# Quantising the feed-forward input in two vector passes instead of three

## The chip, the cores and the metric

The kernel runs on all eight cores of one Trainium2 chip. Each core takes two of the 16 sequences (8192 tokens of 1024 features) and works alone; nothing is exchanged. The time is the device time of the slowest core, in microseconds (us).

## The reference

One layer: a state-space block, a residual and a layer norm, then a quantised feed-forward, a residual and a layer norm.

```python
def fixed_quant(x, width, frac_width):
    scale = 2.0 ** frac_width
    return clip(round(x * scale), -2 ** (width - 1), 2 ** (width - 1) - 1) / scale

x = layernorm(x + ssm(x))                       # (16, 4096, 1024), eps = 1e-5
h = einsum(fixed_quant(x, 8, 4), fixed_quant(w1, 8, 6)) + fixed_quant(b1, 8, 6)
h = relu(fixed_quant(h, 8, 4))                  # hidden size 4096
y = einsum(fixed_quant(h, 8, 4), fixed_quant(w2, 8, 6)) + fixed_quant(b2, 8, 6)
x = layernorm(x + y)
```

Activations are rounded to sixteenths and clipped to -128/16 .. 127/16; weights and biases are rounded to 64ths.

## The kernel before

Features lie on the 128 partitions, tokens along the free dimension. The instruction order of each engine is written out by hand, with a wait on a semaphore wherever a value crosses engines or a buffer comes free. Rounding is done by adding and subtracting MAGIC = 1.5 x 2^23 in float32.

**First stage** (up to some 850 us): 16 blocks of 512 tokens through the state-space block; the residual sum r1 goes to DRAM (r1s) in bfloat16.

**Weights** (some 860 to 1005 us): w1 and w2 are loaded in float32 and quantised by VectorE (DVE) into w1q and w2q in three passes of 4096 columns (L456, L460, L464).

**Feed-forward loop**: 32 blocks of 256 tokens, in a software pipeline. One iteration `it` works on three blocks: t1 = it + 1 (first layer norm LN1 and quantising of x1), t2 = it (up projection by w1) and t3 = it - 1 (down projection by w2, residual, second layer norm LN2). In the steady state TensorE (PE) does in this order:

1. LN1's column sums of r1 and of its squares for t1 (16 matmuls);
2. the down projection of t3, eight groups of 32 matmuls; after the fourth, the two broadcasts of LN1's mean and reciprocal deviation (L540, L545);
3. LN2's column sums for t3 (16 matmuls, L617 to L624), into two PSUM banks of their own;
4. the up projection of t2, 32 groups of eight matmuls; after the 28th, the broadcasts of LN2's rows.

VectorE does in this order: three short instructions on one row for LN1 (L513, L518, L523); one residual sum per down-projection group (L596); LN1 applied to eight chunks of x1 (L554 subtract, L560 multiply); the quantising of x1 into xq_sb, in two halves of four chunks with three passes each (L648, L653, L659); the row instructions for LN2 (L513, L518, L523); then for each four groups of the up projection three passes (L708 out of PSUM, L715, L723) into hq_sb; and last LN2 applied to the eight chunks of the output (L554, L560). ScalarE makes the squares (L505, L603) and, for either norm, rstd = exp(-0.5 ln(var + eps)) on a row (L529, L532).

Banks: `take_bank` deals out banks 0 to 5 in turn, and a bank taken again waits for whoever read it last; banks 6 and 7 are for the broadcasts. After LN2's sums the up projection gets four banks and then the two of the sums, which DVE frees with L513 and L523. The next down projection waits for the last L723 (`hq_vd`). A line L219 or L216 is the helper `mm_group`, which issues most matmuls (L216 the last one of a group).

Scales before the change: x1 is kept at its own scale, in float32, and multiplied by 16 in the first quantising pass; xq and hq hold integers (16 times the value), w1q and w2q hold the rounded weight over 16 (integer/1024), so that both projections come out at the value's own scale.

Of the kernel before, what the change touches and what calls it, by code (L numbers as in the profile page):

```python
# [7 lines left out]
F32 = mybir.dt.float32  # L8
BF16 = mybir.dt.bfloat16
AF = mybir.ActivationFunctionType  # L10
ALU = mybir.AluOpType
# [6 lines left out]
HID = 4096  # L18
# [8 lines left out]
MAGIC = 12582912.0  # L27
EPS = 1e-5
# [6 lines left out]
def build_nc(debug=False):  # L35
# [37 lines left out]
    def sb(name, shape, dtype, region, at=None):  # L73
        if at is None:
            off = (ptr[region] + 31) // 32 * 32
            ptr[region] = off + nbytes_pp(shape, dtype)
        else:
            off = at
        assert off + nbytes_pp(shape, dtype) <= SB_TOP, (name, off)
        h = nc.alloc_sbuf_tensor_at(name, shape, dtype, offset=off)  # L80
        handles[name] = (h, off)
        return h
# [7 lines left out]
    ones_bf = sb("ones_bf", [128, 1], BF16, "P")  # L90
    cb_one = sb("cb_one", [128, 1], F32, "P")
    cb_eps = sb("cb_eps", [128, 1], F32, "P")
    ones_row = sb("ones_row", [1, 128], F32, "P")
    rows1 = tuple(sb("row1_%d" % i, [1, 256], F32, "P") for i in range(4))
    rows2 = rows1
# [50 lines left out]
    with contextlib.ExitStack() as st:  # L146
# [27 lines left out]
        def op(eng, fn, inc=None, inck=1):  # L174
            if inc is None:
                emit(eng, fn)
                return None
            cnt[inc] += inck
            emit(eng, lambda E, f=fn, s=sems[inc], k=inck: f(E).then_inc(s, k))
            return cnt[inc]  # L180
# [64 lines left out]
        op("V", lambda E: E.memset(ones_bf[:], 1.0))  # L245
        op("V", lambda E: E.memset(ones_row[:], 1.0))
        op("V", lambda E: E.memset(cb_one[:], 1.0))
        cv = op("V", lambda E: E.memset(cb_eps[:], EPS), inc="vd")
        wait("S", "qw", qw_all)
        wait("S", "vd", cv)  # L250
        op("S", lambda E: E.activation(out=tmpc1[:], in_=vecs_sb[:, 1:2], func=AF.Exp))
# [21 lines left out]
            return v  # L273

        quant_cols(b1q16, vecs_sb[:, 10:42], 1.0 / 64.0)
        quant_cols(b2q, vecs_sb[:, 42:50], 1.0 / 64.0)
        op("V", lambda E: E.memset(ztmp8[:, 0, 0:1], 0.0), inc="vd")

        dbgA_qs = [0]
# [162 lines left out]
        wq_loads = []  # L442
        first_stage = True

        def stage_quant(dst_ap, src_ap, ncols, si, shape4=False):
            nonlocal first_stage
            pre = list(endA) if first_stage else []
            if len(wq_loads) >= 2:
                pre.append(("vd", wq_loads[-2][1]))
            first_stage = False  # L450
            stg = wstage4[si] if shape4 else wstage[si]
            qv = dma("Y", "qt%d" % si, stg[:, 0:ncols] if not shape4 else stg[:, :, :],
                     src_ap, pre=pre)
            wait("V", "qt%d" % si, qv)
            sap = stg[:, :, :] if shape4 else stg[:, 0:ncols]
            v = op("V", lambda E, s=sap: E.tensor_scalar(  # L456
                out=s, in0=s, scalar1=64.0, scalar2=MAGIC,
                op0=ALU.mult, op1=ALU.add), inc="vd")
            wait("V", "vd", v, selfdep=True)
            v = op("V", lambda E, s=sap: E.tensor_scalar(  # L460
                out=s, in0=s, scalar1=MAGIC, scalar2=127.0,
                op0=ALU.subtract, op1=ALU.min), inc="vd")
            wait("V", "vd", v, selfdep=True)
            vv = op("V", lambda E, s=sap, d=dst_ap: E.tensor_scalar(  # L464
                out=d, in0=s, scalar1=-128.0, scalar2=1.0 / 1024.0,
                op0=ALU.max, op1=ALU.mult), inc="vd")
            wq_loads.append((qv, vv))

# [4 lines left out]
        for k4 in range(HC // 4):  # L473
            stage_quant(w2q[:, 4 * k4:4 * k4 + 4, :],
                        w2T.rearrange("(k p) e -> p k e", p=128)[:, 4 * k4:4 * k4 + 4, :],
                        HID, k4 % 2, shape4=True)
        wq_done = wq_loads[-1][1]

        r1_load = [None] * NTB
# [27 lines left out]
                    inc="sd")  # L507
            state[n]["sq1_sd"] = sqv

        def rows_and_s(bm, bv, tv_m, tv_v, rows):  # L510
            mr, tr, vr, rr = rows
            wait("V", "tm", tv_m)
            vv = op("V", lambda E, b=bm, mr=mr: E.tensor_scalar(  # L513
                out=mr[0:1, :], in0=row_slice(b, TB), scalar1=1.0 / D,
                scalar2=None, op0=ALU.mult, op1=ALU.bypass), inc="vd")
            free_bank(bm, "vd", vv)
            wait("V", "vd", vv, selfdep=True)
            vv = op("V", lambda E, mr=mr, tr=tr: E.tensor_tensor(  # L518
                out=tr[0:1, :], in0=mr[0:1, :], in1=mr[0:1, :],
                op=ALU.mult), inc="vd")  # L520
            wait("V", "tm", tv_v)
            wait("V", "vd", vv, selfdep=True)
            vv = op("V", lambda E, b=bv, tr=tr, vr=vr: E.scalar_tensor_tensor(  # L523
                out=vr[0:1, :], in0=row_slice(b, TB), scalar=1.0 / D,
                in1=tr[0:1, :], op0=ALU.mult, op1=ALU.subtract), inc="vd")
            free_bank(bv, "vd", vv)
            rows_vd = vv
            wait("S", "vd", rows_vd)
            op("S", lambda E, tr=tr, vr=vr: E.activation(  # L529
                out=tr[0:1, :], in_=vr[0:1, :], func=AF.Ln, bias=cb_eps[0:1, :]))  # L530
            drn("S")
            sv = op("S", lambda E, tr=tr, rr=rr: E.activation(  # L532
                out=rr[0:1, :], in_=tr[0:1, :], func=AF.Exp, scale=-0.5), inc="sd")
            return rows_vd, sv

        def emit_bcasts(rows, rows_vd, sv):
# [28 lines left out]
        for it in range(-1, NTB + 1):  # L565
# [4 lines left out]
            if do1:  # L570
                p1 = t1 % 2
                wait("T", "qy%d" % p1, r1_load[t1])
                wait("T", "vd", wq_done)
                if "sq1_sd" not in state[t1]:
                    emit_sq1(t1)
                src1 = [r1ld[:, p1, c, :] for c in range(DC)]
                dst1 = [x1_sb[:, p1, c, :] for c in range(DC)]
                bm1, tvm1 = mm_group([(ones_bf[:], src1[c]) for c in range(DC)],
                                     lambda b: row_slice(b, TB))
                bv1, tvv1 = mm_group([(ones_bf[:], sqb1[:, c, :]) for c in range(DC)],  # L580
                                     lambda b: row_slice(b, TB),
                                     pre_waits=[("sd", state[t1]["sq1_sd"])])
                r1ld_free_T[t1] = max(tvm1, tvv1)
                rows1_vd, sv1 = rows_and_s(bm1, bv1, tvm1, tvv1, rows1)
            if do3:
                p3 = t3 % 2
                st3 = state[t3]
# [44 lines left out]
            if do1:  # L632
                if do3:
                    wait("V", "vd", r2_vd, selfdep=True)
                apply1_vd = emit_apply(src1, dst1, bmb1, brs1, tvrs1)
                r1ld_free_V[t1] = apply1_vd
                if debug and t1 == 0:
                    dma("Y", "qd", dbg["x10"].rearrange("(c p) t -> p c t", p=128),
                        x1_sb[:, 0, :, :], pre=[("vd", apply1_vd)])
                if debug and t1 == 1:  # L640
                    wait("V", "qd", cnt["qd"])
                wait("V", "vd", apply1_vd, selfdep=True)
                for half in range(2):
                    wait("V", "vd", prev_htmp_v[0], selfdep=True)
                    wait("V", "sd", prev_htmp_s[0])
                    for j in range(4):
                        c = half * 4 + j
                        v = op("V", lambda E, c=c, j=j, p=p1: E.tensor_scalar(  # L648
                            out=htmp8b[:, j, :], in0=x1_sb[:, p, c, :], scalar1=16.0,
                            scalar2=MAGIC, op0=ALU.mult, op1=ALU.add), inc="vd")  # L650
                    wait("V", "vd", v, selfdep=True)
                    for j in range(4):
                        v = op("V", lambda E, j=j: E.tensor_scalar(  # L653
                            out=htmp8b[:, j, :], in0=htmp8b[:, j, :], scalar1=MAGIC,
                            scalar2=127.0, op0=ALU.subtract, op1=ALU.min), inc="vd")
                    wait("V", "vd", v, selfdep=True)
                    for j in range(4):
                        c = half * 4 + j
                        xq_vd = op("V", lambda E, c=c, j=j, p=p1: E.tensor_scalar(  # L659
                            out=xq_sb[:, p, c, :], in0=htmp8b[:, j, :], scalar1=-128.0,  # L660
                            scalar2=None, op0=ALU.max, op1=ALU.bypass), inc="vd")
                    prev_htmp_v[0] = xq_vd
                state[t1]["xq_vd"] = xq_vd
                if t1 + 2 < NTB:
                    load_r1(t1 + 2)
            ln2_rows = [None]
            if do3:
                ln2_rows[0] = rows_and_s(bm2, bv2, tvm2, tvv2, rows2)

            def emit_ln2_rows():  # L670
                rows2_vd, sv2 = ln2_rows[0]
# [150 lines left out]
```

How the kernel before makes its waits and increments, by code:

```python
        def wait(eng, sem, val, force=False, selfdep=False):  # L161
            if val is None or val <= 0:
                return
            if not force and not selfdep and own_sem.get(eng) == sem:
                return
            if not force and waited[eng].get(sem, 0) >= val:
                return
            waited[eng][sem] = max(waited[eng].get(sem, 0), val)
            emit(eng, lambda E, s=sems[sem], v=val: E.wait_ge(s, v))
# [4 lines left out]
        def op(eng, fn, inc=None, inck=1):  # L174
            if inc is None:
                emit(eng, fn)
                return None
            cnt[inc] += inck
            emit(eng, lambda E, f=fn, s=sems[inc], k=inck: f(E).then_inc(s, k))
            return cnt[inc]
```

## Time and profile before

| | us |
|---|---|
| median of three timed runs | 3506.78 |
| lowest and highest of them | 3428.13, 3526.78 |
| the profiled execution | 3429.99 |
| its span on the slowest core (core 1) | 3428.4 |
| spans of the eight cores | 3403.0 to 3428.4 |
| PE busy with matmuls | 2869.7 (84%) |
| DVE busy | 2017.1 (59%) |
| ScalarE busy | 462.6 (13%) |

PE's busy share is high in both loops, but it counts a matmul at the lower clock as busy for twice as long, and it is an average over stretches in which PE waits for nobody and stretches in which it waits for DVE. What an edit is worth has to be read from the stretch in which it lies. The granted clock is given as a share of full speed: 1 is 2.4 GHz, 0.5 is 1.2 GHz.

### The profile page before, as it was taken

What the parts mean: (1) busy time and instruction counts of PE and PEld (TensorE: products, weight loads), DVE (VectorE), ACT (ScalarE), POOL (GpSimd) and SP (SyncE); (2) the same over time, 40 slices, a digit from 0 to 9 for tenths busy, and PEclk for the clock granted to TensorE, in tenths of its full rate; (3) what the DMA queues carried; (4) which work ended last, traced back from release to release, by engine and by line L of the source; (5) the groups of instructions that cost most, each with busy time, mean ns of one, the idle gap of its engine ahead of it and who ended that gap; (6) DMA issues with size and microseconds to landing.
All of it is one profiled execution on the core that took longest, in us unless ns stands there. A gap on an engine that the chain in (4) does not pass through costs nothing.

```text
span 3428.4 us, 55367 instructions; the slowest of 8 cores (3403.0 to 3428.4 us)
## 1 busy us (share of the span) xinstructions
PE 2869.7 (84%) x21120; PEld 2099.6 (61%) x21120; DVE 2017.1 (59%) x5836; ACT 462.6 (13%) x979; POOL 19.0 (1%) x26
## 2 busy tenths in 40 slices
PE   2999999998018888888888888888888888888888
PEld 0444444443006677777677777767777776777776
DVE  0343344344676767765777765676776666676655
ACT  0322322331000100011010011101001101100100
POOL 0000000000000000000000000000000000000000
PEclk9999999999558999999999999999999998999999
DMA  8121222120650000000000000000001000000000
GB/s 120 25 44 31 50 50 42 33 50 25 233 190 7 26 19 20 23 28 20 26 19 20 20 32 19 20 26 20 20 19 32 20 20 26 19 20 20 26 13 26
DMA packets 109811, 128.10 MB, mean 37 GB/s; under 512 B 3936, under 2 KB 102240, under 8 KB 108528
## 3 DMA queue, kind: packets, MB, share of 16 engines
q1 hardware_dynamic: 71936, 83.89, 7.4%
q0 software_dynamic: 20976, 23.89, 5.2%
q10 hardware_dynamic: 16640, 16.78, 1.8%
q8 instruction: 173, 2.83, 0.3%
q14 instruction: 86, 0.70, 0.1%
HBM read 98.07 MB, written 50.33 MB: 43 GB/s over the span
## 4 chain that ended last, share of the span: by engine, by line
PE 74%; DVE 18%; issue 2%; DMA 2%; another core or an unknown queue 2%; ACT 0%; DVEq 0%; ACTq 0%; SPq 0%
PE pb L219 65%; PE pb L216 7%; DVE x_sb L560 3%; DVE x_sb L554 3%; DVE htmp8b L708 2%; DVE htmp8b L653 2%; DVE htmp8b L648 2%; DVE xq_sb L659 2%; DVE htmp8b L715 1%; DVE hq_sb L723 1%; PE pb L540 1%; DMA wstage_b<-w2T 1%; PE pb L545 1%; DMA wstage_a<-w1T 1%
## 5 line engine op out<-in xcount | busy, mean ns | idle before, releaser
L219 PE MATMUL pb<-xq_sb,w1q 128*128 128x256 bf16 x7168 | 973.3, 286 | 218.9 <-DVE row L513 214.3
L219 PE MATMUL pb<-hq_sb,w2q 128*128 128x256 bf16 x7936 | 920.5, 277 | 72.0 <-DVE hq_sb L723 72.0
L219 PEld LDWEIGHTS pb<-xq_sb,w1q 128*128 128x128 bf16 x7168 | 726.1, 102 | 355.2 <-issue 238.4
L219 PEld LDWEIGHTS pb<-hq_sb,w2q 128*128 128x128 bf16 x7936 | 783.0, 99 | 190.3 <-issue 90.4
L596 DVE SCALAR_TENSOR_TENSOR r_sb<-pb,b2q,x_sb 128x256 bf16<-128x256 f32 x256 | 123.1, 481 | 647.6 <-PE pb L216 647.5
L219 PE MATMUL pb<-xb,winT_sb 128*128 128x512 bf16 x1792 | 435.2, 383 | 68.1 <-DMA xb<-xT 64.8
L708 DVE TENSOR_SCALAR htmp8b<-pb,b1q 128x256 f32<-128x256 f32 x1024 | 426.8, 476 | 50.7 <-DVE hq_sb L723 26.3
L219 PEld LDWEIGHTS pb<-xb,winT_sb 128*128 128x128 bf16 x1792 | 175.7, 99 | 285.1 <-issue 89.1
L216 PE MATMUL pb<-xq_sb,w1q 128*128 128x256 bf16 x1024 | 289.8, 283 | 0.0
L723 DVE TENSOR_SCALAR hq_sb<-htmp8b 128x256 bf16<-128x256 f32 x1024 | 230.6, 289 | 28.1 <-DVE htmp8b L715 0.9
L715 DVE TENSOR_SCALAR htmp8b<-htmp8b 128x256 f32<-128x256 f32 x1024 | 230.7, 289 | 27.8 <-DVE htmp8b L708 0.5
L390 DVE TENSOR_TENSOR r_sb<-pb,xb 128x512 bf16<-128x512 f32 x128 | 88.6, 692 | 243.0 <-PE pb L216 243.0
L529 ACT ACTIVATE row<-row,cb_eps 1x256 f32<-1x256 f32 x64 | 32.6, 510 | 1436.9 <-DVE row L523 1423.9
L219 PE MATMUL pb<-z_sb,woutT_sb 128*128 128x512 bf16 x896 | 215.8, 381 | 8.7 <-DVE z_sb L418 8.7
L603 ACT ACTIVATE sqb<-r_sb 128x256 bf16<-128x256 bf16 x256 | 104.4, 415 | 722.7 <-DVE r_sb L596 722.6
L219 PEld LDWEIGHTS pb<-z_sb,woutT_sb 128*128 128x128 bf16 x896 | 88.0, 98 | 115.6 <-issue 10.9
L219 PE MATMUL pb<-r1ld,ones_bf 128*1 128x256 bf16 x224 | 31.1, 281 | 145.7 <-DMA r1ld<-r1s 145.7
L342 DVE TENSOR_SCALAR ld_t<-sp_t,negrate 128x512 f32<-128x512 f32 x16 | 7.8, 486 | 229.3 <-ACT sp_t L338 229.3
L321 ACT CAST u_bf<-pb 128x512 bf16<-128x512 f32 x128 | 75.1, 587 | 398.6 <-PE pb L216 398.6
L216 PEld LDWEIGHTS pb<-xq_sb,w1q 128*128 128x128 bf16 x1024 | 104.2, 102 | 15.7
L219 PEld LDWEIGHTS pb<-r1ld,ones_bf 128*1 128x1 bf16 x224 | 16.6, 85 | 157.8 <-issue 153.2
L505 ACT ACTIVATE sqb<-r1ld 128x256 bf16<-128x256 bf16 x256 | 81.6, 401 | 185.6 <-DMA r1ld<-r1s 185.6
(93 smaller groups left out, 1855.2 us busy)
## 6 DMA issues: line engine op xcount, KB each, us to landing
outT<-ob SPq DMA_DIRECT2D x32, 1024.0 KB, 4.5
xb<-xT POOLq DMA_DIRECT2D x16, 1024.0 KB, 13.3
r1s<-r_sb ACTq DMA_DIRECT2D x16, 1024.0 KB, 6.4
r1ld<-r1s SPq DMA_DIRECT2D x32, 512.0 KB, 4.1
wstage_a<-w1T SPq DMA_DIRECT2D x4, 2048.0 KB, 8.1
wstage_b<-w1T SPq DMA_DIRECT2D x4, 2048.0 KB, 8.2
wstage_a<-w2T SPq DMA_DIRECT2D x4, 2048.0 KB, 8.6
wstage_b<-w2T SPq DMA_DIRECT2D x4, 2048.0 KB, 8.6
```

The source lines that it names most:

```text
L216: E.matmul(o, l, r, **kw), inc="tm")
L219: E.matmul(o, l, r, **kw))
L321: sv = op("S", lambda E, b=b, e=e, p=par: E.copy(out=u_bf[:, p, e, :], in_=full(b)), inc="sd")
L390: vv = op("V", lambda E, b=b, e=e, p=parp, xp=tp % 3: E.tensor_tensor(out=r1_sb[:, p, e, :], in0=full(b), in1=xb[:, xp, e, :], op=ALU.add) ...
L505: sqv = op("S", lambda E, c=c, p=p: E.activation(out=sqb1[:, c, :], in_=r1ld[:, p, c, :], func=AF.Square), inc="sd")
L554: E.tensor_tensor(out=d, in0=s, in1=ln_slice(b, TB), op=ALU.subtract), inc="vd")
L560: E.tensor_tensor(out=d, in0=d, in1=ln_slice(b, TB), op=ALU.mult), inc="vd")
L596: r2_vd = op("V", lambda E, b=b, e=e, p=p3: E.scalar_tensor_tensor(out=r2_sb[:, e, :], in0=ln_slice(b, TB), scalar=b2q[:, e:e + 1], in1=x1 ...
L603: sq2_sds.append(op("S", lambda E, e=e: E.activation(out=sqb2[:, e, :], in_=r2_sb[:, e, :], func=AF.Square), inc="sd"))
L708: v = op("V", lambda E, b=b, hc=hc, j=j: E.tensor_scalar(out=htmp8b[:, j, :], in0=ln_slice(b, TB), scalar1=b1q16[:, hc:hc + 1], scalar2=16 ...
L715: v = op("V", lambda E, j=j: E.tensor_scalar(out=htmp8b[:, j, :], in0=htmp8b[:, j, :], scalar1=MAGIC, scalar2=MAGIC, op0=ALU.add, op1=ALU. ...
L723: v = op("V", lambda E, j=j, hc=hc: E.tensor_scalar(out=hq_sb[:, hc, :], in0=htmp8b[:, j, :], scalar1=127.0, scalar2=0.0, op0=ALU.min, op1 ...
```

## The change

x1 is now kept at 16 times its scale, so that quantising it needs no multiplication. LN1's rstd is made 16 times larger by a bias of ln 16 in the exponential. The first quantising pass adds and subtracts MAGIC, the second clips on both sides; the pass at L653 is gone. So that the residual sum fits, w2 is stored as integer/64 instead of integer/1024 and b2 is 16 times larger; LN2 then sees 16 times its input, and gets 256 times the epsilon, so its output is as before. Two small constant tiles are added.

```diff
+        op("V", lambda E: E.memset(cb_eps256[:], 256.0 * EPS))
+        cv = op("V", lambda E: E.memset(cb_ln16[:], float(np.log(16.0))), inc="vd")
...
-        quant_cols(b2q, vecs_sb[:, 42:50], 1.0 / 64.0)
+        quant_cols(b2q, vecs_sb[:, 42:50], 16.0 / 64.0)
...
         for k4 in range(HC // 4):
             stage_quant(w2q[:, 4 * k4:4 * k4 + 4, :],
                         w2T.rearrange("(k p) e -> p k e", p=128)[:, 4 * k4:4 * k4 + 4, :],
-                        HID, k4 % 2, shape4=True)
+                        HID, k4 % 2, shape4=True, postmul=16.0 / 1024.0)
...
+                sv = op("S", lambda E, tr=tr, rr=rr, eb=exp_bias: E.activation(
+                    out=rr[0:1, :], in_=tr[0:1, :], func=AF.Exp,
+                    scale=-0.5, bias=eb[0:1, :]), inc="sd")
...
-                rows1_vd, sv1 = rows_and_s(bm1, bv1, tvm1, tvv1, rows1)
+                rows1_vd, sv1 = rows_and_s(bm1, bv1, tvm1, tvv1, rows1,
+                                           exp_bias=cb_ln16)
...
                     for j in range(4):
                         c = half * 4 + j
                         v = op("V", lambda E, c=c, j=j, p=p1: E.tensor_scalar(
-                            out=htmp8b[:, j, :], in0=x1_sb[:, p, c, :], scalar1=16.0,
-                            scalar2=MAGIC, op0=ALU.mult, op1=ALU.add), inc="vd")
-                    wait("V", "vd", v, selfdep=True)
-                    for j in range(4):
-                        v = op("V", lambda E, j=j: E.tensor_scalar(
-                            out=htmp8b[:, j, :], in0=htmp8b[:, j, :], scalar1=MAGIC,
-                            scalar2=127.0, op0=ALU.subtract, op1=ALU.min), inc="vd")
+                            out=htmp8b[:, j, :], in0=x1_sb[:, p, c, :],
+                            scalar1=MAGIC, scalar2=MAGIC,
+                            op0=ALU.add, op1=ALU.subtract), inc="vd")
                     wait("V", "vd", v, selfdep=True)
                     for j in range(4):
                         c = half * 4 + j
                         xq_vd = op("V", lambda E, c=c, j=j, p=p1: E.tensor_scalar(
-                            out=xq_sb[:, p, c, :], in0=htmp8b[:, j, :], scalar1=-128.0,
-                            scalar2=None, op0=ALU.max, op1=ALU.bypass), inc="vd")
+                            out=xq_sb[:, p, c, :], in0=htmp8b[:, j, :],
+                            scalar1=127.0, scalar2=-128.0,
+                            op0=ALU.min, op1=ALU.max), inc="vd")
...
-                ln2_rows[0] = rows_and_s(bm2, bv2, tvm2, tvv2, rows2)
+                ln2_rows[0] = rows_and_s(bm2, bv2, tvm2, tvv2, rows2,
+                                         eps_ap=cb_eps256)
```

## Rows read from the trace of the kernel before

**Rows 1.** The page's first line: the span of the slowest core.
```profile
span 3428.4 us, 55367 instructions; the slowest of 8 cores (3403.0 to 3428.4 us)
```

**Rows 2.** Chain of waits, first matmuls of down projections: start, length (us), what.
```profile
1076.05 5.21 PE pb L219 x31
...
2045.67 3.54 PE pb L219 x31
...
2120.45 5.21 PE pb L219 x31
...
2196.10 5.16 PE pb L219 x31
...
2495.62 3.54 PE pb L219 x31
...
2569.30 3.54 PE pb L219 x31
...
3316.88 6.24 PE pb L219 x31
```

**Rows 3.** Timeline, PE, iteration of 2045.67: start, length, instructions, [idle before, releaser].
```profile
2080.31 0.27 PE L216 MATMUL pb<-xq_sb,w1q 128*128 128x256 bf16 x1
2087.73 1.65 PE L219 MATMUL pb<-xq_sb,w1q 128*128 128x256 bf16 x7 [7.14 <-DVE row L513]
...
2094.09 0.93 PE L219 MATMUL pb<-xq_sb,w1q 128*128 128x256 bf16 x7
...
2120.45 5.21 PE L219 MATMUL pb<-hq_sb,w2q 128*128 128x256 bf16 x31 [2.24 <-DVE hq_sb L723]
```

**Rows 4.** Timeline, PE, iteration of 2495.62: its opening, and from the end of the stall.
```profile
2495.62 3.54 PE L219 MATMUL pb<-hq_sb,w2q 128*128 128x256 bf16 x31 [1.89 <-DVE hq_sb L723]
...
2537.67 1.65 PE L219 MATMUL pb<-xq_sb,w1q 128*128 128x256 bf16 x7 [7.16 <-DVE row L513]
...
2540.92 0.93 PE L219 MATMUL pb<-xq_sb,w1q 128*128 128x256 bf16 x7
```

**Rows 5.** Timeline, DVE, iteration of 2045.67, from quantising into the up projection.
```profile
2081.33 0.90 DVE L648 TENSOR_SCALAR htmp8b<-x_sb 128x256 f32<-128x256 f32 x4
2082.34 0.90 DVE L653 TENSOR_SCALAR htmp8b<-htmp8b 128x256 f32<-128x256 f32 x4
2083.34 0.90 DVE L659 TENSOR_SCALAR xq_sb<-htmp8b 128x256 bf16<-128x256 f32 x4
...
2087.18 0.41 DVE L513 TENSOR_SCALAR row<-pb 1x256 f32<-1x256 f32 x1
...
2094.36 0.48 DVE L708 TENSOR_SCALAR htmp8b<-pb,b1q 128x256 f32<-128x256 f32 x1 [0.71 <-PE pb L216]
...
2104.73 1.66 DVE L708 TENSOR_SCALAR htmp8b<-pb,b1q 128x256 f32<-128x256 f32 x4 [0.18 <-PE pb L216]
...
2108.58 1.66 DVE L708 TENSOR_SCALAR htmp8b<-pb,b1q 128x256 f32<-128x256 f32 x4 [0.18 <-DVE hq_sb L723]
```

**Rows 6.** Waits, 1070 to 3317 us: who for whom, us in total, times, longest.
```profile
PE pb L219 <- DVE row L513: 214.3, 30, 7.4
PE pb L219 <- DVE hq_sb L723: 67.7, 31, 4.3
...
DVE htmp8b L708 <- PE pb L216: 17.2, 63, 1.0
```

**Rows 7.** Instructions by tile: count, ns min/median/max; last, DVE's groups: count, busy us, mean ns.
```profile
L653 DVE TENSOR_SCALAR htmp8b<-htmp8b x256: 284/287/295, 1024.6 to 3283.5; 128x256 f32<-128x256 f32 x128
...
L529 ACT ACTIVATE row<-row,cb_eps x64: 509/510/511, 1015.5 to 3415.7; 1x256 f32<-1x256 f32 x64
L532 ACT ACTIVATE row<-row x64: 417/417/420, 1016.1 to 3416.3; 1x256 f32<-1x256 f32 x64
...
L248 DVE MEMSET cb_eps<- 128x1 f32 x1 | 0.1, 59 | 0.0
```

**Rows 8.** One stretch of the first stage: us, PE busy, granted clock (PEclk), DMA.
```profile
208.56:212.43 3.87, 3.87 (x17) 0.81 0.52 86
```

More of the change, by code:

```diff
@@ L92, in build_nc @@
     cb_eps = sb("cb_eps", [128, 1], F32, "P")
+    cb_eps256 = sb("cb_eps256", [128, 1], F32, "P")
+    cb_ln16 = sb("cb_ln16", [128, 1], F32, "P")
     ones_row = sb("ones_row", [1, 128], F32, "P")
@@ L247, in build_nc @@
         op("V", lambda E: E.memset(cb_one[:], 1.0))
-        cv = op("V", lambda E: E.memset(cb_eps[:], EPS), inc="vd")
+        op("V", lambda E: E.memset(cb_eps[:], EPS))
+        op("V", lambda E: E.memset(cb_eps256[:], 256.0 * EPS))
+        cv = op("V", lambda E: E.memset(cb_ln16[:], float(np.log(16.0))), inc="vd")
         wait("S", "qw", qw_all)
@@ L443, in build_nc, with stage_quant @@
         first_stage = True
-        def stage_quant(dst_ap, src_ap, ncols, si, shape4=False):
+        def stage_quant(dst_ap, src_ap, ncols, si, shape4=False,
+                        postmul=1.0 / 1024.0):
             nonlocal first_stage
@@ L463, in stage_quant @@
             wait("V", "vd", v, selfdep=True)
-            vv = op("V", lambda E, s=sap, d=dst_ap: E.tensor_scalar(
-                out=d, in0=s, scalar1=-128.0, scalar2=1.0 / 1024.0,
+            vv = op("V", lambda E, s=sap, d=dst_ap, pm=postmul: E.tensor_scalar(
+                out=d, in0=s, scalar1=-128.0, scalar2=pm,
                 op0=ALU.max, op1=ALU.mult), inc="vd")
@@ L508, in emit_sq1, with rows_and_s @@
             state[n]["sq1_sd"] = sqv
-        def rows_and_s(bm, bv, tv_m, tv_v, rows):
+        def rows_and_s(bm, bv, tv_m, tv_v, rows, eps_ap=None, exp_bias=None):
+            if eps_ap is None:
+                eps_ap = cb_eps
             mr, tr, vr, rr = rows
@@ L528, in rows_and_s @@
             wait("S", "vd", rows_vd)
-            op("S", lambda E, tr=tr, vr=vr: E.activation(
-                out=tr[0:1, :], in_=vr[0:1, :], func=AF.Ln, bias=cb_eps[0:1, :]))
+            op("S", lambda E, tr=tr, vr=vr, ep=eps_ap: E.activation(
+                out=tr[0:1, :], in_=vr[0:1, :], func=AF.Ln, bias=ep[0:1, :]))
             drn("S")
-            sv = op("S", lambda E, tr=tr, rr=rr: E.activation(
-                out=rr[0:1, :], in_=tr[0:1, :], func=AF.Exp, scale=-0.5), inc="sd")
+            if exp_bias is None:
+                sv = op("S", lambda E, tr=tr, rr=rr: E.activation(
+                    out=rr[0:1, :], in_=tr[0:1, :], func=AF.Exp,
+                    scale=-0.5), inc="sd")
+            else:
+                sv = op("S", lambda E, tr=tr, rr=rr, eb=exp_bias: E.activation(
+                    out=rr[0:1, :], in_=tr[0:1, :], func=AF.Exp,
+                    scale=-0.5, bias=eb[0:1, :]), inc="sd")
             return rows_vd, sv
```

## The prediction

> **What bounds the kernel now.** I read the page's first lines, then the chain of waits, then the timelines of TensorE (PE) and VectorE (DVE) over single iterations of the feed-forward loop, then the waits, and last the groups of the lines that are edited. The span is 3428.4 us [rows 1]; the profiled execution itself took 3429.99 us, 1.6 us outside the span, and all sums below are made against that 3430 us. It is close to the lowest of the three timed runs (3428.13); their median is 3506.78, 2.2% higher. The same saving counted from the median would end about 77 us higher than my number; I keep my number at the profiled execution.
>
> The feed-forward loop opens its first down projection (w2) at 1076.05 us and its 31st at 3316.88 us [rows 2]: 30 iterations in 2240.83 us, 74.69 us each. Inside one iteration the bound changes hands. During the down projection PE runs without a gap and DVE waits for it. At its end DVE starts a long serial piece: normalise x1, quantise it into xq, then the three statistic rows, and only then does it read the PSUM banks again. PE meanwhile does four groups of the up projection (w1), finds the next bank still held by the statistics, and stands for 7.14 us until DVE's L513 [rows 3, 6]. From there DVE is behind for good: it takes 3.85 us for four chunks (L708 at 2104.73 and at 2108.58 [rows 5]), where PE needs about 3.6 us for four groups of eight matmuls (a down-projection group of 31 such matmuls took 3.54 us [rows 2]). So PE finishes the up projection first and waits once more, 2.24 us, for the last hq chunks before the next down projection [rows 3]. Summed over the 30 iterations PE waited 214.3 us for L513 and 67.7 us for L723 [rows 6]. Hence the time from DVE's first normalising instruction to its last L723 is DVE's, and whatever is taken out of DVE's line there comes off the iteration.
>
> **The change part by part.** (a) Quantising x1 goes from three passes of eight instructions to two; L653 disappears. Starts of consecutive half passes are 2081.33, 2082.34, 2083.34 [rows 5], so four instructions with their wait cost 1.005 us, and an iteration loses two such half passes: 2.01 us. The group's mean, 285 to 295 ns each [rows 7], is longer than the spacing because the instructions overlap; the spacing is the price. L653 ran 256 times, eight per block over 32 blocks [rows 7]. All of them are on the path: 30 in the iterations above, and two before the first opening, where nothing else runs. Direct: 32 x 2.01 = 64.3 us.
>
> The two passes that remain keep their shapes (128x256 f32 to f32, and to bf16). The last pass now has min and max as L723 does, and L723 lasts as long as L653 and L659; I take no change for it. Bounds: nothing, or in the other direction the slowest read of this shape against the fastest, 295 against 284 ns, which over 512 instructions would be 5.6 us.
>
> (b) Scale by 16 moved into the exponent of LN1: ScalarE's L532 gets a bias column. L529 of the same size already has one and takes 510 ns against 417 ns without [rows 7] (part of that may be Ln against Exp), so at most 0.1 us on a chain that ends well before its reader. LN1's rows are made at the start of the down projection and broadcast after its fourth group: the cover is four groups of 3.54 us. Without it the price would be 32 x 0.1 = 3 us; only the first two blocks have none. (c) Other constants in the weight quantisation, in b2 and in the second epsilon: same instruction count, same shapes, nothing. (d) Two more memsets of 59 ns [rows 7] while the first weights load: nothing. (e) Two small tiles move everything behind them by 64 bytes per partition: I take nothing, and can bound it only by whatever is left over.
>
> Is there still a stall to shorten? PE stands 7.14 us; it would stand 5.13 us, so the cover is not used up. Late next is the same DVE line: the up projection stays at DVE's 3.85 us per four chunks.
>
> (f) The clock. After every one of the 30 stalls at L513 the clock was at its lower level, 1.2 GHz: the first group of eight matmuls after the stall took 1.65 us for seven where 0.93 us is the full-clock figure [rows 3, 4]. In the iteration of 2045.67 the slow stretch reached from 2087.73 to about 2093.6 us, and DVE had to wait for PE (0.71 us at 2094.36 [rows 5]); in the iteration of 2495.62 it was over by 2540.92, and DVE never waited. Read off the same chain, the 30 iterations are of three kinds: 7 without any delay, 73.67 to 73.96 us (2495.62 to 2569.30 [rows 2]); 12 with DVE delayed in the up projection, 74.3 to 74.8 us; and 11 in which the 1.9 to 2.5 us wait ahead of the down projection made the clock fall and its first group took 5.21 instead of 3.54 us, about 75.5 us (2120.45 to 2196.10 [rows 2]). Against 73.7 us for all, the clock costs 2240.83 - 30 x 73.7 = 29.8 us: 11 x 1.67 = 18.4 us in the openings and 11.4 us in the delays. The waits of L708 for PE, 17.2 us in all [rows 6], bound the second part from above.
>
> What does a stall of 5.13 us do? No row shows one. The neighbours are 7.14 us (lower clock always) and 1.9 to 2.5 us (in a third of the cases). With the stall 2 us shorter PE resumes sooner, and I expect the slow stretch behind it to be no longer than that of the iteration of 2495.62, 3.25 us, which did not delay DVE, rather than the 5.9 us of 2045.67, which did. So I take the delays as gone (11.4 us). Eight of the 12 delayed iterations are followed by a slow opening (the one of 2045.67 by that of 2120.45 [rows 2, 3]), for a late DVE makes the wait ahead of the down projection longer, 2.24 against 1.89 us [rows 3, 4]; three of the 11 slow openings come otherwise. So with the delays most slow openings should go, and I take six of 11, 10 us. Together a rounded 20 us. The bounds are 29.8 us gained (every iteration 71.7 us) and 24 us lost (every opening slow: 30 x 0.99 us becomes 30 x 1.8 us).
>
> Sum: 3430 - 64 - 20 = 3346 us, a ratio of 1.025.
>
> By a page of notes the direct part would be smaller: the Trainium skill, VectorE: DVE Perf Modes, in the section on the TRN2 errata, gives a single-source VectorE instruction between SBUF tiles 58 cycles plus elements over the mode's factor, at 0.96 GHz (an estimate of 194 ns for 256 elements at two per cycle). By that the direct part would be 256 x 0.194 = 50 us and the sum 3360 us. The trace's 1.005 us for four, wait included, decides here.
>
> **Rivals.**
> - *The clock gives nothing back.* Shorter stalls still end in slow stretches as long as today's, and the average excess of 0.99 us per iteration stays. For it: the lower clock followed even waits of 2.2 us. Against it: the clean iterations already have most of the stall. Time: 3430 - 64 = 3366 us, 1.9% faster, within what I call no change.
> - *The clock gets worse.* The phase of the shorter loop puts the wait ahead of the down projection where the clock falls every time. Time: 3366 + 24 = 3390 us.
> - *The removed pass was cover.* The stall would have to end with something other than DVE, or the compiler would keep the time elsewhere. The waits put all 30 stalls on L513 [rows 6], so little speaks for it. Time: 3430 us.
> - *The other side: a denser PE trips a power limit.* The granted clock was 0.81 for 3.87 us at 208.56 [rows 8], in the first stage, with PE busy throughout; in the loop the opening groups stand at 3.5 or 5.2 us and not near 3.54/0.81 = 4.4 us [rows 2], so there it did not act. In the loop 34.9 us of each iteration, from the opening at 2045.67 to the start of the stall at 2087.73 - 7.14 [rows 2, 3], go at PE's own speed. At 0.81 they would take 34.9 x 0.235 = 8.2 us longer, 246 us over 30. It decides from a share of 64/246 = 26% of that time; held throughout, the time is 3366 + 246 = 3612 us. The Trainium skill, TensorE: Matmul & The Clock Gate, Part 1, says that three dense cores of a die bring the clock to 13/16 and hold it there while the load lasts; by that rule the 3612 us would come. This trace shows the 0.81 in stretches of 4 to 5 us only, with eight busy cores. The change takes 2 us of idle from 74.7 us, which makes PE hardly denser.
>
> **How the numbers follow.** Forecast 0.62; clock unchanged 0.20; clock worse 0.08; removed pass covered 0.04; limiter 0.04; something unforeseen 0.02. The predicted time is 3346 us. The likeliest case alone runs from 3330 us (64 + 30, with 6 us for cores and chips: the eight spans differ by 25 us) to 3362 us. The range has to reach to the unchanged clock and the worse one; I let it go from 3325 to 3425 us, which also takes in the case that the result is told from runs like the median of before (3507 - 84 = 3423 us). A measurement of this kernel tells about 2% from no change, here 3361 us. Faster by over 2%: nearly all of the forecast and a little of the second case, 0.64. Within 2%: 0.31. Slower by over 2%: 0.05.
>
> **What the next profile would show.** DVE with 254 instructions fewer (256 less the two memsets) and about 70 us less busy; PE's wait for L513 at 5.1 us, 155 us over 30; iterations of mostly 71.7 us; the wait of L708 for PE near nothing; slow openings about five instead of 11. The prediction is wrong if the wait for L513 stays near 7 us (pass was covered), if iterations of 73 us and more are common (clock), if L648 or L659 grow, or if opening groups stand near 4.4 us (limiter).

## The result and the profile after

The changed kernel takes 0.975 of the time of the kernel before (95% interval 0.9735 to 0.9764). Its profiled execution took 3342.83 us against 3429.99 us, its median is 3342.57 us over nine runs, and that of the kernel before 3516.78 us over ten. The ratio compares undisturbed runs alone; the two medians don't, because some executions of either kernel are slowed by a lower clock on a whole die (more of those before than of those after), and where that fell into a profiled execution only the other die's cores are read below.

The page of the changed kernel, first line and the busy times (us, share of the span, instructions):

```profile
span 3341.3 us, 55049 instructions; the slowest of 8 cores (3325.1 to 3341.3 us)
...
PE 2839.5 (85%) x21120; PEld 2085.4 (62%) x21120; DVE 1957.5 (59%) x5582; ACT 463.1 (14%) x979; POOL 19.0 (1%) x26
```

DVE has 254 instructions fewer (5836 to 5582), as the edit says, and 60 us less busy. Both spans can be cut at the first and at the 31st opening of the down projection. Of the chain of waits of the changed kernel, start, length and what it is (rows 2 of before answer to these):

```profile
1075.49 5.07 PE pb L221 x31
...
1149.44 3.54 PE pb L221 x31
...
2082.13 3.54 PE pb L221 x31
...
2153.78 3.54 PE pb L221 x31
...
2225.45 3.54 PE pb L221 x31
...
3229.68 4.88 PE pb L221 x31
```

Up to the first opening 0.6 us were gained (1076.05 to 1075.49), in the 30 iterations 86.6 us (2240.83 to 2154.19, so 74.69 to 71.81 us each), and behind the 31st opening nothing (111.5 and 111.6 us). All of the gain is in the loop. Of the 30 openings one is slow, the first; before it were 11 [rows 2]. The iteration of 2153.78 takes 71.67 us, and 27 of the 30 lie between 71.59 and 71.99 us.

PE in that iteration (start, length, instructions, idle before and its releaser), beside [rows 3, 4]:

```profile
2153.78 3.54 PE L221 MATMUL pb<-hq_sb,w2q 128*128 128x256 bf16 x31 [1.89 <-DVE hq_sb L736]
...
2193.82 1.65 PE L221 MATMUL pb<-xq_sb,w1q 128*128 128x256 bf16 x7 [5.13 <-DVE row L521]
...
2195.48 1.70 PE L221 MATMUL pb<-xq_sb,w1q 128*128 128x256 bf16 x7
...
2197.18 1.44 PE L221 MATMUL pb<-xq_sb,w1q 128*128 128x256 bf16 x7
...
2198.57 0.93 PE L221 MATMUL pb<-xq_sb,w1q 128*128 128x256 bf16 x7
```

DVE in the same iteration, beside [rows 5]:

```profile
2189.44 0.90 DVE L663 TENSOR_SCALAR htmp8b<-x_sb 128x256 f32<-128x256 f32 x4
2190.44 0.90 DVE L670 TENSOR_SCALAR xq_sb<-htmp8b 128x256 bf16<-128x256 f32 x4
2191.45 0.90 DVE L663 TENSOR_SCALAR htmp8b<-x_sb 128x256 f32<-128x256 f32 x4
2192.45 0.90 DVE L670 TENSOR_SCALAR xq_sb<-htmp8b 128x256 bf16<-128x256 f32 x4
2193.27 0.41 DVE L521 TENSOR_SCALAR row<-pb 1x256 f32<-1x256 f32 x1
```

From the first quantising pass to the row instruction L521 there are 3.83 us, where there were 5.85 (2081.33 to 2087.18): 2.02 us. PE's stall went from 7.14 to 5.13 us. The clock is at its lower level after this stall too (1.65 and 1.70 us for seven matmuls, 0.93 from 2198.57 on), for 4.7 us, and DVE isn't delayed by it. The moments at which the granted clock changed can be cut out as well. Stretches just ahead of and behind three falls in a row of the same core (us, PE busy, PEclk, DMA share, GB/s):

```profile
1187.37:1187.87 0.50, 0.00 (x0) 1.00 1.13 344
1187.87:1188.37 0.50, 0.00 (x0) 0.50 0.82 246
1259.05:1259.55 0.50, 0.00 (x0) 1.00 1.08 312
1259.55:1260.05 0.50, 0.00 (x0) 0.50 1.13 343
1330.73:1331.23 0.50, 0.00 (x0) 1.00 0.91 262
1331.23:1331.73 0.50, 0.00 (x0) 0.50 1.14 341
```

The clock fell at 1187.87, 1259.55 and 1331.23 us, 71.68 us apart both times.

Waits of the 30 iterations, 1070 to 3230 us, beside [rows 6]:

```profile
PE pb L221 <- DVE row L521: 155.4, 30, 5.5
PE pb L221 <- DVE hq_sb L736: 65.2, 31, 4.0
```

### The profile page after: what moved, and what is told of

Its sections match the earlier page's. It is cut to its first block, busy times and chain, and to the rows that moved or that the text cites. A ratio compares the mean times of both kernels' runs of the same rounds, so it can differ in the third digit from the quotient of the medians.

```text
span 3341.3 us, 55049 instructions; the slowest of 8 cores (3325.1 to 3341.3 us)
## 1 busy us (share of the span) xinstructions
PE 2839.5 (85%) x21120; PEld 2085.4 (62%) x21120; DVE 1957.5 (59%) x5582; ACT 463.1 (14%) x979; POOL 19.0 (1%) x26
## 4 chain that ended last, share of the span: by engine, by line
PE 76%; DVE 17%; DMA 3%; issue 2%; another core or an unknown queue 2%; ACT 0%; DVEq 0%; ACTq 0%; SPq 0%
PE pb L221 67%; PE pb L218 7%; DVE x_sb L568 3%; DVE x_sb L574 3%; DVE htmp8b L721 2%; DVE htmp8b L663 2%; DVE xq_sb L670 2%; DVE htmp8b L728 1%; DVE hq_sb L736 1%; DMA wstage_a<-w2T 1%; DMA wstage_a<-w1T 1%; PE pb L554 1%; PE pb L559 1%; DVE wstage_a L465 1%
## 5 line engine op out<-in xcount | busy, mean ns | idle before, releaser
L221 PE MATMUL pb<-hq_sb,w2q 128*128 128x256 bf16 x7936 | 903.5, 274 | 69.7 <-DVE hq_sb L736 69.7
L221 PEld LDWEIGHTS pb<-hq_sb,w2q 128*128 128x128 bf16 x7936 | 774.5, 98 | 179.5 <-issue 88.1
L221 PE MATMUL pb<-xb,winT_sb 128*128 128x512 bf16 x1792 | 431.2, 381 | 65.6 <-DMA xb<-xT 62.2
## 6 DMA issues: line engine op xcount, KB each, us to landing
wstage_b<-w2T SPq DMA_DIRECT2D x4, 2048.0 KB, 10.3
```

The source lines that it names most:

```text
L221: E.matmul(o, l, r, **kw))
```

## The experiments

In the tables and sentences below an iteration is the time from one down-projection opening to the next; "shortest" and "mean" are over the 30 of one core, and a range is over the cores of the profiled execution. The mean less the shortest is what the clock costs in an iteration: its slow openings, and DVE's delays in the up projection. "Slow" is an opening whose first 31 matmuls ran wholly or partly at the lower clock. Each kernel was profiled once, so the ranges show how the cores of one execution differ. The traces of all kernels, in order of the stall:

| kernel | stall us | shortest us | mean us | clock cost us | slow openings of 30 |
|---|---|---|---|---|---|
| before | 7.14 | 73.6 | 74.3 to 74.7 | 0.7 to 1.0 | 6 to 11 |
| changed, third pass back | 7.14 | 73.6 | 74.3 to 74.5 | 0.7 to 0.9 | 6 to 8 |
| before, 13 idle matmuls | 7.13 | 75.0 | 75.25 to 75.6 | 0.3 to 0.6 | 2 to 5 |
| changed, third pass in one half | 6.14 | 72.6 | 73.4 to 73.7 | 0.9 to 1.1 | 7 to 11 |
| changed | 5.13 | 71.6 | 71.7 to 71.8 | 0.15 to 0.2 | 1 |
| changed, 9 idle matmuls | 5.13 | 72.5 | 72.9 to 73.15 | 0.35 to 0.6 | 1 to 4 |
| one pass in one half (cores 0 to 3) | 4.12 | 70.6 | 71.4 to 71.6 | 0.9 to 1.0 | 9 to 15 |
| one pass | 3.11 | 69.6 | 70.7 to 71.0 | 1.1 to 1.5 | 13 to 22 |
| one pass, 18 idle matmuls | 3.11 | 71.5 | 71.7 to 72.0 | 0.2 to 0.5 | 1 to 5 |

**The third pass put back.** On the changed kernel, between the two passes:

```diff
                     wait("V", "vd", v, selfdep=True)
+                    if True:
+                        for j in range(4):
+                            v = op("V", lambda E, j=j: E.tensor_scalar(
+                                out=htmp8b[:, j, :], in0=htmp8b[:, j, :],
+                                scalar1=127.0, scalar2=-128.0,
+                                op0=ALU.min, op1=ALU.max), inc="vd")
+                        wait("V", "vd", v, selfdep=True)
```

> The changed kernel with a third pass of the removed one's shape put back (a second, idle clip to -128..127 in htmp8b, 256 instructions); the scales stay as changed. Theory A (a half pass of four instructions costs the 1.005 us that its starts show, and the clock part goes with the waits as such): the time of the kernel before, ratio 1.00, 74.7 us per iteration. Theory B (the clock changes its level at moments of its own, so what it costs hangs on where the loop's period puts the waits): the same, 1.00, because the period is that of before. If the new scales, biases or the moved tiles carried any of the gain, the ratio would be below 0.995.

Measured: ratio 0.9998 (0.9986 to 1.001), stall 7.14 us, mean 74.3 to 74.5 us. The new scales, the biases and the tiles moved by 64 bytes bring or cost nothing beyond that interval; the gain is the absence of 256 instructions and of the wait behind each four of them.

**Half of it put back, and two steps further.** The second kernel has `if half == 0:` in place of `if True:`. The other two leave the first pass out instead, in the second half or in both (there the clip reads x1 directly, so this x1 is clipped but not rounded to sixteenths):

```diff
-                            out=xq_sb[:, p, c, :], in0=htmp8b[:, j, :],
+                            out=xq_sb[:, p, c, :], in0=htmp8b[:, j, :] if r else x1_sb[:, p, c, :],
```

> The third pass put back in the first half only, so DVE's line is 1.0 us longer than in the changed kernel and 1.0 us shorter than before. Theory A: halfway or a little better, 72.8 us per iteration and ratio 0.983 to 0.987. Theory B: the period near 72.7 us does not put the waits at a harmless place each time, most openings are slow again: 73.9 to 74.4 us per iteration, ratio 0.993 to 0.998, so that the second half pass is worth several times the first.

> Going on in the same direction: the second half is no longer rounded (its first pass is left out, the clip reads x1 directly), so DVE's line is another 1.0 us shorter. Theory A: 70.7 us per iteration, ratio 0.965. Theory B: slow openings come back and eat it: about 71.7 us per iteration, ratio 0.973 to 0.976, as the changed kernel.

> Neither half is rounded: the rounding of x1 is left out and only the clip remains, so DVE's line is 2.0 us shorter than in the changed kernel, and the stall at the banks 3.1 us. Theory A: 69.7 us per iteration, ratio 0.956. Theory B: still about 71.6 us, every opening slow (5.2 us), ratio 0.972 to 0.976.

Measured: 0.9915 (0.9888 to 0.9943), 0.9722 (0.97 to 0.9745) and 0.966 (0.9635 to 0.9685). The shortest iteration falls by one even step per half pass: 73.6, 72.6, 71.6, 70.6, 69.6 us. So DVE's line is the bound throughout, and four instructions are worth 1.0 us each time. The mean doesn't follow in even steps. With the kernel before at 1 and the changed one at 0.975, the first half pass brings 0.85%, the second 1.65%, the third 0.3% and the fourth 0.6% (by the intervals each is good to about 0.3 points, so the third is barely told from nothing; the means of the traces fall by 0.9, 1.9, 0.2 and 0.7 us). Theory A is too low each time, by 0.6 to 0.9 us for the first (it had 72.8), 0.7 to 0.9 for the second and 1.0 to 1.3 for the third; theory B has its direction right each time and its size in one of three (its 71.6 us for the last is 0.6 to 0.9 too high, its 73.9 for the first 0.2 to 0.5).

The kernel with one pass has the shortest stall and yet the most slow openings. Of core 2's chain of waits, some of its 22 from 1131.47 to 3120.73 us:

```profile
1131.47 5.21 PE pb L221 x31
1203.10 5.21 PE pb L221 x31
1274.68 5.21 PE pb L221 x31
1346.10 5.21 PE pb L221 x31
...
3120.73 5.21 PE pb L221 x31
```

Its waits, core 2, 1050 to 3330 us:

```profile
PE pb L221 <- DVE row L521: 92.5, 30, 3.2
PE pb L221 <- DVE hq_sb L738: 79.2, 32, 4.5
```

The wait for L521 fell to 3.1 us each, that ahead of the opening stayed at about 2 to 2.5 us, and it is the second that now costs the clock.

**The period moved without DVE.** To tell the length of the stall from the period of the loop, idle matmuls were put ahead of the sixth down-projection group, where PE is the bound; they write the bank that the group then starts over:

```diff
             n = len(lhs_rhs)
+            for lhs, rhs in lhs_rhs[:idle_mms]:
+                op("T", lambda E, l=lhs, r=rhs, o=out_ap(b):
+                   E.matmul(o, l, r, start=True, stop=True))
```

> The changed kernel with nine idle matmuls (0.98 us at 0.109 us each) in the sixth down-projection group of every block; they write the bank that the group then starts over. DVE's line and the 5.13 us stall are as in the changed kernel; only the loop's period is 1.0 us longer, near that of the kernel with a third pass in one half. Theory A (the shorter stall as such is what made the clock harmless): shortest iteration 72.6 us, mean 72.8 us, ratio 0.984. Theory B (the period decides): shortest 72.6 us, but slow openings and delays are back, mean 73.4 to 73.8 us, ratio 0.989 to 0.993.

> The kernel without the rounding of x1 (which is left out here too) with 18 idle matmuls, 1.96 us, in every block. Its shortest iteration becomes 71.5 us, next to the changed kernel's 71.6. Theory A: its mean of 70.9 us grows by the whole work to 72.8 us, ratio 0.983. Theory B: the slow openings (13 to 22 of 30 without the matmuls) nearly all go, as in the changed kernel, mean 71.6 to 71.9 us, ratio 0.973 to 0.976, so that 2 us of added work cost under 1 us.

> The kernel before with 13 idle matmuls, 1.42 us, in every block: the stall stays at 7.14 us and the shortest iteration becomes 75.1 us. Theory A: mean 74.65 + 1.42 = 76.1 us, ratio 1.013. Theory B, if the loop falls into step here too: mean 75.1 to 75.4 us, ratio 1.004 to 1.007, most of the added work free although the stall is as long as before.

Changed kernel with nine of them: the profiled execution took 3382.04 us; there is no ratio with an interval, so the trace speaks alone. Mean 72.9 to 73.15 us: the 0.95 us of work cost 1.1 to 1.4 us. Neither theory's number was met: A had 72.8 and is the nearer, B 73.4 to 73.8. Slow openings stay rare, but 11 to 13 of the 30 iterations of a core are more than 0.45 us over the shortest, where the changed kernel has one or two; most of them are delays of DVE in the up projection.

One pass with 18 of them: ratio 0.9802 (0.9754 to 0.9849), A had 0.983 and B 0.973 to 0.976, so the times don't decide. The trace does: A had a mean of 72.8 us, B 71.6 to 71.9, and 71.7 to 72.0 were measured. The stall is as without the matmuls (92.2 against 92.5 us), but of core 3's chain these are all the openings of over 5 us:

```profile
1070.00 5.21 PE pb L224 x31
...
1289.15 5.21 PE pb L224 x31
...
2511.12 5.21 PE pb L224 x31
...
3295.83 5.21 PE pb L224 x31
```

```profile
PE pb L224 <- DVE row L524: 92.2, 30, 3.2
PE pb L224 <- DVE hq_sb L742: 80.3, 32, 4.5
```

(Second fence: its waits, 1050 to 3330 us. Two more openings, at 1215.11 and 2437.01 us, lie partly at the lower clock, which makes the five of the table.) With the same waits in number and length, the matmuls took the slow openings from 13 to 22 down to 1 to 5, and 1.96 us of added work cost 0.8 to 1.3 us per iteration (core 4: 70.96 to 71.74 us; core 0: 70.67 to 71.97 us).

Kernel before with 13: ratio 1.011 (1.0086 to 1.0134). By the times A's 1.013 is within the interval and B's 1.004 to 1.007 isn't; by the trace the clock cost fell from 0.7 to 1.0 us to 0.3 to 0.6, half of what B asked, with the stall unchanged (213.6 us over 30).

Taken together: at one stall length the clock cost changes by a factor of two to five with the period (5.13 us: 0.2 and 0.5; 3.11 us: 1.3 and 0.3; 7.14 us: 0.9 and 0.4). At nearly one period, 72.6 and 72.5 us, it changes with the stall as well (6.14 us: 1.0; 5.13 us: 0.5), but that pair differs in the idle matmuls too, so the stall's own part is less sure than the period's.

What the period does can be read from the moments of the clock itself. Take the 68 cores read for this table, from 1050 to 3300 us. All 2485 falls of the granted clock to 1.2 GHz lie within 3 ns of an even grid of times, one grid per core, with the same step in every kernel. So do the rises, all but eight (one per core of the kernel with one pass). PE's waits decide at which marks the clock falls, but they don't move the marks. In the changed kernel, from 1120 to 3000 us on eight cores, 188 of the 200 spaces between one fall and the next are 71.68 us, which is a whole number of steps and next to its iteration of 71.6 to 71.7 us. In the kernel with one pass and 18 idle matmuls it is 185 of 214, in the kernel before 72 of 254.

The place on the grid also sorts waits of one length. Ahead of 1262 openings of the table's kernels PE stood 2.0 to 2.6 us. Of those that began in one half of the grid's step 336 of 361 were slow, of those in the other half 9 of 901. (The ends of the half were picked from these same openings; of the waits of 2.2 to 2.3 us alone, 152 of 153 against 1 of 170.) So what sets the changed kernel apart is that each of its iterations puts its two waits where the one before had them on this grid, at a harmless place; a loop with another period drifts over it and meets the harmful half again and again. Why a wait is harmful in one half and not in the other no run here takes apart.

**ScalarE takes the pass out of PSUM.** If DVE's line is the bound, work has to leave DVE. ScalarE evacuates the up projection's banks into htmp8b (it reads them out of PSUM into SBUF); LN2's rows go ahead of the quantising of x1, ob serves as scratch for it, and LN1's squares are spread over the up projection. Of the edit, the evacuation alone:

```diff
-                        wait("V", "tm", tv)
-                        v = op("V", lambda E, b=b, hc=hc, j=j: E.tensor_scalar(
-                            out=htmp8b[:, j, :], in0=ln_slice(b, TB),
-                            scalar1=b1q16[:, hc:hc + 1], scalar2=16.0,
-                            op0=ALU.add, op1=ALU.mult), inc="vd")
-                        free_bank(b, "vd", v)
+                        wait("S", "tm", tv)
+                        wait("S", "vd", slot_v[j])
+                        sv = op("S", lambda E, b=b, hc=hc, j=j: E.activation(
+                            out=htmp8b[:, j, :], in_=ln_slice(b, TB),
+                            func=AF.Identity, scale=16.0,
+                            bias=b1q16[:, hc:hc + 1]), inc="sd")
+                        free_bank(b, "sd", sv)
```

> A candidate to beat both. On the changed kernel, ScalarE (13% busy) takes the first pass out of PSUM (L708 before) from DVE, in an activation with scale 16 and bias 16 b1; LN2's rows go ahead of the quantising of x1, which uses ob as its scratch so that htmp8b is free; LN1's squares are spread over the up projection. DVE's up-projection line falls from 3.85 to about 2.1 us per four chunks, below PE's 3.5. If DVE's line was the whole bound of that phase, PE becomes the bound: stall at the banks under 2 us, iteration 65.5 to 67.5 us, ratio 0.91 to 0.93. If ScalarE's evacuations (about 0.5 us each) or its waits for htmp8b pace it instead, 68 to 70 us, ratio 0.94 to 0.96.

> The kernel with ScalarE's evacuations once more, as the partner of the next one on the same chip: ratio 0.914 to 0.920, 65.2 to 65.4 us per iteration.

Measured: 0.9166 (0.9138 to 0.9195) and, again, 0.9133 (0.91 to 0.9166); the profiled execution of the second took 3125.28 us. Every iteration lies between 65.2 and 65.6 us on every core, and from 1120 to 3000 us the clock never falls. PE's waits in one iteration, by the timeline of its second run:

```profile
2008.26 0.93 PE L221 MATMUL pb<-xq_sb,w1q 128*128 128x256 bf16 x7 [1.31 <-DVE row L531]
...
2014.50 0.92 PE L221 MATMUL pb<-xq_sb,w1q 128*128 128x256 bf16 x7 [0.67 <-ACT htmp8b L737]
```

The 5.13 us stall has become 1.3 and 0.7 us, and the wait ahead of the opening is nearly gone (under 0.5 us). This is the version that beats both kernels. Two parts of the edit can have shortened the long stall: DVE reads the statistics' banks before it quantises x1, and its line in the up projection is shorter. They were not run apart, so how much ScalarE's taking the pass brings by itself isn't shown.

**The same pass once more, on that version.** The third pass put back, in ob, for all eight chunks:

```diff
+                for c in range(DC):
+                    v = op("V", lambda E, c=c: E.tensor_scalar(
+                        out=ob[:, c, :], in0=ob[:, c, :],
+                        scalar1=127.0, scalar2=-128.0,
+                        op0=ALU.min, op1=ALU.max), inc="vd")
+                wait("V", "vd", v, selfdep=True)
```

> The same with the removed third pass put back on DVE (256 more instructions, about 1.9 us more of DVE's line in every block). If a pass is worth its time only while DVE's line sets the iteration, it now costs under 0.4 us per iteration, ratio within 0.004 of its partner's. If ScalarE's wait for htmp8b, and with it PE's second wait at the banks, is pushed out by the pass, 1 to 2 us per iteration, ratio 0.013 to 0.025 above the partner's.

Measured: 0.9412 (0.9384 to 0.944), 0.028 above its partner; mean 68.2 to 68.3 against 65.3 us. I had leaned to "free", and it costs 3.0 us for 1.9 us of instructions, more than the upper case of 2. PE in one iteration:

```profile
1992.77 0.93 PE L221 MATMUL pb<-xq_sb,w1q 128*128 128x256 bf16 x7 [1.36 <-DVE row L531]
...
2000.84 1.58 PE L221 MATMUL pb<-xq_sb,w1q 128*128 128x256 bf16 x7 [2.49 <-ACT htmp8b L743]
```

The wait for ScalarE's evacuation grew from 0.67 to 2.49 us: ScalarE can't write htmp8b before DVE has read it, DVE comes 1.8 us later, and the pass lies on the path as before. After 2.49 us of standing the clock falls, in 21 to 23 of the 30 iterations; those take 68.5 to 69.1 us, the others 67.05 (one 67.3), so about 1.6 us each and 1.2 us in the mean. 1.8 and 1.2 are the 3.0 us.

## Why the prediction was right or wrong

**Bound.** Right. DVE's line sets the time from the first normalising instruction to the last L723; the shortest iteration followed it in steps of 1.0 us over five kernels, and 30 waits of each still end with DVE's row.

**Part (a), direct.** Right in size: 2.02 us per block measured, 2.01 predicted, 60 us over the 30 iterations. (DVE's busy time fell by 60 us, where I had about 70.) The two passes ahead of the first opening should have brought 4 us more; 0.6 came on the slowest core. The weight loads that stand in front of it landed in 9.2 to 10.3 us where they took 8.1 to 8.6, and cores differ by 13 to 14 us at this point. In the mean of the eight cores the first opening comes 1.9 us sooner, and whether the slower loads took the rest isn't shown. L663 and L670 run 285 to 295 ns, as L653 did [rows 7]. The 1.005 us between starts was the right price. Its parts are in the same rows: four instructions fill 0.90 us and one lasts 0.287 us, so inside a group they start 204 ns apart ((0.90 - 0.287)/3), and the 0.19 us that are left of 1.005 are DVE waiting for its own last write. The formula of the Trainium skill, VectorE: DVE Perf Modes, in the section on the TRN2 errata, gave an estimate of 194 ns, which fits the spacing inside a group; the 50 us made of it were too few because the wait of each group wasn't in them.

**Parts (b) to (e).** Right: the third pass put back gives 0.9998. ScalarE's exponential with a bias takes 507 ns against 415 without, hidden.

**Part (f), the clock.** The sum was right, 26 us measured (29.8 us of clock cost down to 3.5, on a base of 73.7 less 2.01, 71.69 us) against 20 predicted, but the mechanism behind it was not. I had it that a shorter stall makes the delays vanish, and with them most slow openings, and that six of 11 would go. Ten went. The slow stretch behind the stall was to be no longer than 3.25 us; it lasts 4.7 us and delays nothing. What fails is the step that ties the clock's cost to the length of the stall: at 6.14 us of stall there were still 7 to 11 slow openings and a clock cost of 1.0 us, and at 4.12 and 3.11 us there were more slow openings, 9 to 15 and 13 to 22 where the kernel before has 6 to 11. By my step these kernels should have been cleaner than the changed one. The step left out the period of the loop and the grid on which the clock changes, which the runs showed in its place: 188 of 200 falls follow one another at 71.68 us. Half of the pass would have hinted at it: half the work brought a third of the gain. My second rival, in which the phase of the shorter loop puts the wait at a bad place, had the right mechanism and the wrong sign; here the place of the waits was luck, worth 0.7 to 0.9 us in every iteration.

**The sum and the range.** Against the profiled execution 3346 us stands beside 3342.83. As a change from the median of before it doesn't hold: 0.975 of 3516.78 us is 3428.9 us, 3.9 us over the top of my range. The step of the sum that failed is the one that set that top. I took it as 3507 less 84 and two us, with no room for another median: the medians of before were 3506.78 over three runs and 3516.78 over ten, and for the reason given with the result such a median can move by more than the effect that I sized (the same kernel had medians of 3422.6 to 3431 us beside the experiments). And 3346 set against 3506.78 would read as 4.6% faster, where the kernel is 2.5% faster. The forecast should have been carried through as a ratio, 0.9755, and the time's range made as wide as the runs shown, 3428 to 3527, times that ratio: 3344 to 3441 us and on from there by the cases.

**Rivals.** Clock gives nothing back (3366): no, 26 us of it came. Clock gets worse (3390): not here, but one half pass further it began, and the kernel with one pass has 13 to 22 slow openings. Pass was cover (3430): no. Limiter (3612): the loop's openings stand at 3.54 us, and the mean granted clock over it is 0.95 where it was 0.94; the rule of the Trainium skill, TensorE: Matmul & The Clock Gate, Part 1, that three dense cores bring 13/16 for as long as the load lasts, isn't borne out by this profiled execution, whose loop has no stretch at 0.81 with eight busy cores.

## What to carry to other kernels

Find the engine whose serial line is the iteration, price an edit by the spacing of starts on that line, and check whether a loop that is otherwise regular has iterations of two or three lengths; if it has, part of the time is the clock's, and it can go either way with any edit. Then look at the moments at which the granted clock changes. Measure half of the edit and twice the edit before crediting a mechanism: here equal steps of 1.0 us brought 0.3% to 1.65%. Where an engine with 14% of busy time can take a pass from the engine that sets the line, that can be worth more than shortening the pass: 8.3 to 8.7% against 2.5%, here together with a better order of DVE's work.

## What the runs showed of the hardware

Added TensorE work can cost half its length: 1.96 us of idle matmuls in every iteration cost 0.8 to 1.3 us, because slow openings went from 13 to 22 down to 1 to 5, with waits of the same number and length. Waits of 1.9 to 2.5 us were followed by the lower clock in some iterations and not in others of the same kernel, and which ones moved with the loop's period. The Trainium skill, TensorE: Matmul & The Clock Gate, Part 1, says of the monitor that its window "doesn't reset when your kernel starts"; the traces agree: the falls lie within 3 ns of one grid whatever PE waits for, and where the grid's first mark lies behind the kernel's start differs from core to core. The cost of a fall just ahead of an opening is the same in every trace: 5.21 against 3.54 us for the first 31 matmuls, and less where the clock rises again within them.

ScalarE's evacuation of a 128x256 float32 bank with scale and bias took 473 ns (median) against 475 on DVE. A VectorE instruction that waits for VectorE's own last write starts 0.19 us later than one that doesn't (1.005 us from one group of four to the next, 204 ns from one instruction to the next inside it).
